# A four-batch decoder kernel: shorter weight loads and early splits, step products beside a norm, the recurrent mixer as one block, expert weights spread from bf16 rows

## The reference, cut to what matters

```python
x = _layernorm(x + _L0_attn_ref(x, ...))                  # selective-state scan, 1024 channels x 16 states
x = _layernorm(x + _L0_xattn_ref(x, fside, ctx_1024))     # two int8-style quantised linears
x = _layernorm(x + _L0_ffn_ref(x, ...))                   # silu(gate) * up, down, hidden 2048
x = _layernorm(x + _L1_attn_ref(x, ...))                  # recurrent mixer, 32 heads of 8 x 16 states
x = _layernorm(x + _L1_xattn_ref(ctx_1024, x, ...))       # selective-state scan, 512 channels x 16 states
x = _layernorm(x + _L1_ffn_ref(x, ...))                   # 8 routed experts of 352 and a shared one of 1408
```

```python
mus = einsum('blnr,nrd->blnd', tanh((x + delta * mu_x) @ Wx1), Wx2)     # five mixes
r = (x + delta * mr) @ Wr;  k = ... @ Wk;  v = ... @ Wv;  g = ... @ Wg
w = tanh((x + delta * mw) @ Ww1) @ Ww2 + bw;  decay = exp(-exp(w))
S = S * dt[..., :, None] + kv                                           # over 512 times
```

## Time and profile before

| | us |
|---|---|
| median of 3 runs | 4110.94 (4108.12 to 4114.24) |
| the profiled execution's own time | 4114.88 |
| its span, first to last instruction | 4113.1 |
| PE matmul / DVE / ACT / POOL busy in the span | 3610.2 / 3202.9 / 1641.1 / 1277.0 |
| mean granted PE clock | 0.935 |

### The profile page before, as it was taken

The page is one execution under the profiler, slowest core; times in us unless marked ns, Lnnn a source line. Parts: engine busy times, 40 slices in busy tenths (PEclk is TensorE's granted clock), DMA queues, the critical chain, the costliest instruction groups (busy, mean ns, idle before and its releaser), DMA issues. The chain is left out here.

```text
span 4113.1 us, 42098 instructions
## 1 busy us (share of the span) xinstructions
PE 3610.2 (88%) x15651; PEld 1499.2 (36%) x15651; DVE 3202.9 (78%) x2747; ACT 1641.1 (40%) x2207; POOL 1277.0 (31%) x453
## 2 busy tenths in 40 slices
PE   5777779978999979988999979988999979966999
PEld 2222243323433443323433443334333443323444
DVE  5998559768899869868899869778999869775333
ACT  4666443214655343214655353214655343112001
POOL 1444204343244304343244304343344304331000
PEclk9888899989899989989999999989999989977999
DMA  3888502222233402222233302122233302110222
GB/s 148 304 323 298 226 24 77 69 80 82 74 102 96 141 34 77 69 80 82 75 103 102 134 34 85 63 83 78 85 102 101 138 29 77 62 54 16 93 98 74
DMA packets 91354, 418.57 MB, mean 102 GB/s; under 512 B 14224, under 2 KB 26640, under 8 KB 88720
## 3 DMA queue, kind: packets, MB, share of 16 engines
q1 hardware_dynamic: 69552, 378.15, 26.0%
q10 hardware_dynamic: 21600, 37.73, 3.3%
HBM read 320.45 MB, written 70.25 MB: 95 GB/s over the span
## 5 line engine op out<-in xcount | busy, mean ns | idle before, releaser
L276 PE MATMUL ps<-r,ring 128*128 128x512 bf16 (+2 forms) x2040 | 786.5, 386 | 0.0
L1127 POOL TENSOR_TENSOR hh<-hh,bc 128x2048 f32<-128x2048 f32 x72 | 338.5, 4701 | 920.5 <-DVE hh L1047 920.5
L273 PE MATMUL ps<-xr,ring 128*128 128x512 bf16 x1568 | 614.9, 392 | 1.3 <-DVE r L259 1.2
L277 PE MATMUL ps<-xr,ring 128*128 128x512 bf16 x1568 | 613.7, 391 | 0.0
L273 PE MATMUL ps<-r,ring 128*128 128x512 bf16 (+2 forms) x1384 | 548.5, 397 | 63.7 <-DVE xc L1085 15.1
L277 PE MATMUL ps<-r,ring 128*128 128x512 bf16 (+2 forms) x1384 | 548.8, 397 | 0.0
L1127 POOL TENSOR_TENSOR bc<-bc 128x2048 f32<-128x2048 f32 x64 | 297.4, 4647 | 356.1 <-DVE bc L1047 356.1
L1127 POOL TENSOR_TENSOR r<-r,bc 128x2048 f32<-128x2048 f32 x56 | 263.1, 4699 | 325.2 <-DVE r L1047 325.2
L1047 DVE TENSOR_TENSOR_SCAN hh<-da,hh 128x2048 f32<-128x2048 f32 x72 | 330.1, 4585 | 1.3
L1088 DVE TENSOR_TENSOR xc<-xc,ps 128x512 f32<-128x512 f32 x176 | 119.4, 678 | 233.5 <-PE ps L277 233.5
L1047 DVE TENSOR_TENSOR_SCAN bc<-da,bc 128x2048 f32<-128x2048 f32 x64 | 289.6, 4525 | 0.5
(11 more groups left out here) (252 smaller groups left out, 6606.1 us busy)
## 6 DMA issues: line engine op xcount, KB each, us to landing
ring<-wsplit SPq DMA_DIRECT2D x304, 768.0 KB, 4.2
r<-wstream SPq DMA_DIRECT2D x76, 768.0 KB, 6.9
wsplit<-ring SPq DMA_DIRECT2D x58, 768.0 KB, 4.6
da<-r ACTq DMA_DIRECT2D x360, 63.9 KB, 2.0
wsplit<-r SPq DMA_DIRECT2D x18, 768.0 KB, 5.6
r<-xT SPq DMA_DIRECT2D x7, 1024.0 KB, 5.0
r<-gates_dram ACTq DMA_DIRECT2D x3, 2048.0 KB, 9.4
bc<-guwT SPq DMA_DIRECT2D x4, 1024.0 KB, 7.7
```

The costliest lines, as they stand in the source:

```text
L273: mm = pe.matmul(out, w_hi, x_hi, start=start, stop=False)
L276: pe.matmul(out, w_hi, x_lo, start=False, stop=False)
L277: return pe.matmul(out, w_lo, x_hi, start=False, stop=stop)
L1127: pool.tensor_tensor(quartet(s), quartet(s), k.out_rows, ALU.mult).then_inc(read, 1)
```

## The change

1. Used columns. `SLOT_COLUMNS` gives for each slot how many of its 1536 columns are used (1384 on average); ring loads, splitting and stores take only these. In `first_preparation` 8 of the 71 slots (9728 columns) are now split beside the preparation: ACT makes the high parts between its other steps, POOL all the low parts. 63 slots (88256 columns instead of 71 x 1536 = 109056) stay for the first scan stage, by DVE for 21 of them (28224 columns instead of 24 x 1536 = 36864) and PE for 42 (60032 columns in 118 chunks instead of 47 slots in 141).
2. Step products. `dt_product`, `magnitude`, `positive`, `exponential`, `logarithm`, `total` and the eight spread rows of the second scan leave `second_preparation` and go into `norm_and_steps`, which takes the place of `layer_norm` ln1 (and has no `keep_busy`).
3. One block for the mixer. `mix_inputs`, `mix_projections` and `mix_scan` become `mix_batch`. The scan loop starts after two of the four v products; the other two, the four g products and the 16 of the next batch are handed out in the loop, 3, 2, 3, 3, 2, 3, 3 and 3 in its eight steps. The third mix has tiles of its own (`xc`, `held_more`).
4. Weight rows. The expert weights' rows lie as three bf16 parts in 96 partitions, made on POOL at the start of "moe" (four instructions); a spread is one bf16 matmul over 96 rows instead of one f32 matmul over 32, and the first one comes after the first tile's gate and up.

```diff
-                sp.dma_start(self.whole[n % SPLIT_RING], self.source[self.slots[n]]).then_inc(self.landed[n % SPLIT_RING], 16)
+                at = slice(0, self.columns[n])
+                sp.dma_start(self.whole[n % SPLIT_RING][:, at], self.source[self.slots[n]][:, at]).then_inc(self.landed[n % SPLIT_RING], 16)
...
-def first_preparation(nc, k, slot, last):
+def first_preparation(nc, k, slot, last, splitter):
...
+                if j < SPLIT_RING:
+                    splitter.high_part(act, j)
             s.silu(act, J0 - 1)
             s.take_low(act)
             for j in range(J0):
                 s.magnitude(act, j)
+                if j % 2 == 1 and SPLIT_RING + j // 2 < count:
+                    splitter.high_part(act, SPLIT_RING + j // 2)
...
+            for n in range(early):
+                splitter.low_part(pool, n)
             for j in range(J0):
                 s.split_x(pool, j)
+            for n in range(early, count):
+                splitter.low_part(pool, n)
...
-                pe.matmul(weight_bank(e)[a:b, :], k.ident[q:q + 32, q + e:q + e + 1].broadcast_to([32, b - a]),
-                          k.weight_rows[q:q + 32, :], start=True, stop=True).then_inc(spread_mm, 1)
+                pe.matmul(weight_bank(e)[a:b, :], k.stack[0:96, e:e + 1].broadcast_to([96, b - a]),
+                          k.weight_parts, start=True, stop=True).then_inc(spread_mm, 1)
...
+def norm_and_steps(nc, k, tag, parts, slots_end, last):
...
+        @blk.tensor
+        def _(pe):
+            s.dt_product(pe, 0)
+            s.dt_product(pe, 1)
+            norm.means(pe)
+            s.dt_product(pe, 2)
+            s.dt_product(pe, 3)
+            norm.variances(pe)
+            for r in range(2 * GRP):
+                s.spread_row(pe, r)
...
+        @blk.vector
+        def _(dve):
+            norm.sums(dve)
+            s.positive(dve, 0)
+            s.positive(dve, 1)
+            norm.centred(dve)
+            s.positive(dve, 2)
+            s.positive(dve, 3)
+            for r in range(GRP):
+                s.dve_row(dve, r)
+            norm.scaled(dve)
+            for i in range(2):
+                s.total(dve, i)
...
+            value(0)
+            value(1)
             spread(0)
             pe.wait_ge(rb, 2)
...
+            work = [(value, 2), (value, 3)] + [(gate, o) for o in range(4)] + ([(ahead_product, n) for n in range(2 * J0)] if ahead else [])
+            given = 0
             for g in range(G):
                 if g + 1 < G:
                     spread(g + 1)
                 if g >= 1:
                     reduce(g - 1)
-                if ahead:
-                    project(2 * g)
-                    project(2 * g + 1)
+                until = max(len(work) * (g + 1) // G, min(3, len(work)))
+                for which, n in work[given:until]:
+                    which(n)
+                given = until
             reduce(G - 1)
...
+            times(0)
+            times(1)
+            split(0)
+            times(2)
+            split(1)
+            times(3)
+            dve.wait_ge(taken, 3)
+            low(dve, k.lowrank_lo, k.lowrank).then_inc(lsplit, 1)
+            split(2)
+            times(4)
+            split(3)
```

629 lines of the change are left out of this document (334 added, 295 removed).

## The result

| | before | after |
|---|---|---|
| median of the runs, us | 4110.64 (4108.12 to 4114.24, 4 runs) | 3986.22 (3982.17 to 3991.31, 4 runs) |
| span of the profiled execution | 4113.1 | 3980.4 |
| PE matmul / DVE / ACT / POOL busy | 3610.2 / 3202.9 / 1641.1 / 1277.0 | 3521.7 / 3172.7 / 1609.0 / 1378.0 |
| mean granted PE clock | 0.935 | 0.939 |

The ratio is 0.9693, 95% interval 0.9681 to 0.9706. The time forecast was 3981.

What follows compares the result with a forecast made beforehand. Bounds were taken by stage: DVE in the first scan stage and mixer loop, PE in "moe", engines waiting in turn in the mixer's front. Terms 8 - 26 - 37 - 16 + 43 - 58 - 30 - 14 = -130 gave 3981 us, range 3938 to 4030.

Steps and rivals of the forecast that it cites:

- The sum: Whole kernel: all terms together -130 us, giving 3985 in a profiled execution and 3981 as median.
- The second preparations and the norm: Step products move to ln1: second preparations -37 (batches two to four) and -16 (first), four norms +43 us.
- the 20 dummy matmuls were hidden: In ln1: the 20 dummy matmuls that go were hidden, so no term was given for removing them.
- The first scan stage: Fewer slots and 19% fewer columns for DVE, PE and ACT: -26 us, between -10 and -45.
- The first preparation: ACT and POOL split eight slots there, POOL's low parts meeting DVE's taps: +8 us, between +1 and +20.
- The front of the mixer: Mixer before its first scan: multiplications a mix early bring that scan to 54.8 from 86.1 us, -31.
- The loop: Mixer scan loop with a next batch: becomes PE's and ends after 80 instead of 69 us.
- in DVE's slack: Mixer with a next batch: POOL's four low parts of the next x cost about 1 us, in DVE's slack.
- the last batch: Last batch's mixer: loop stays DVE's, first scan at 54.8, 126 instead of 156.1 us, -30 (-20 to -35).
- The weight rows: "moe": bf16 spreads over 96 rows give -2 us in each stage with a scan, -8 in the last, together -14.
- the front keeps its pace: Rival, mixer front: low parts and POOL's additions lock each other out, front 12 us longer, +48, 4029; chance 0.14.
- The lower clock for a whole loop: Rival, mixer loop: PE at the lower clock, products 5.1 instead of 2.76 us, 4135 in all; chance 0.04.

Runs made afterwards that it cites:

- e3: The changed kernel with the step products and spread rows back in the second preparation and the plain norm in their place; 3991.46 us, ratio 0.9704.
- e10: The changed kernel with 30 dummy matmuls behind the spread rows of the norm with the step products; 3989.72 us, ratio 0.9699.
- e1: The changed kernel with all 1536 columns used in every slot again; 3998.21 us, ratio 0.9715.
- e2: The changed kernel with no slot split in the first preparation, all 71 split in the first scan stage; 4008.04 us, ratio 0.9738.
- e7: The changed kernel with the multiplications of each mix directly ahead of its low parts, not a mix early; 4033.07 us, ratio 0.9805.
- e8: The changed kernel with one matmul instead of three for each part of the next batch's 16 products in the mixer loop; 3966.35 us, ratio 0.9642.
- e5: The changed kernel with the low parts of the next batch's x made by DVE ahead of the first mixer scan, not by POOL; 4012.92 us, ratio 0.9753.
- e4: The changed kernel with the expert weights' rows spread in f32 from 32 rows again, without POOL's splitting; 4010.52 us, ratio 0.9743.
- e6: e5 with the second product of v also moved into the mixer loop; 4021.53 us, ratio 0.9773.
- e9: The changed kernel with POOL splitting x after its reads, DVE's read directly behind the scan, and the second v product in the loop; 4008.20 us, ratio 0.9747.
- e11: The changed kernel with both e9's mixer loop order and e10's dummy matmuls; 3985.18 us, ratio 0.9693.

## Why the prediction was right, step by step

*The sum* is nearer than its terms: against the forecast the first preparation came out 5.0 lower and "moe" 7.3 lower, the mixers 9.0 and the first scan stage 1.6 higher. That these cancel to 2.7 is luck; each mechanism below is judged by its own stage. (The profiled execution is also the fastest of the four: the median is 5 above the forecast.)

*The second preparations and the norm* were right to 1.6 us a batch (13.2, 13.2 and 10.6 for 12.2; that they sum to the forecast's 37 is luck too) and to 0.1 in the norm, because all of it was counted from rows of these stages: 36 products at 5.52 for 24, ACT's functions and DVE's four operations by name. What was wrong is the sentence that the 20 dummy matmuls were hidden: they cost nothing where they stood, but the stage behind them pays for their absence (177.7 for 176.0 to 177.6 before and 176.0 to 177.5 in e3, part of it back in e10).

*The first scan stage* came out at -24.4 for -26. From scan to scan it takes 10.0 us in its first half and 10.4 in its second (10.3 and 11.6 before), which was to come under 10.6. e1 and e2 show that the parts had other sizes: the eight early slots give 14.5, the narrower columns 7.4.

*The first preparation* was oversized, +3.0 for +8. POOL's 19.6 us were priced as four pieces in the way of DVE's taps and 3.5 us of ACT; in fact they met little: DVE's busy time grew by 3.6, and POOL's is 30.5, 2.0 more than its 8.95 of before and the 19.6. "SBUF — State Buffer" of the Trainium skill, section "Who interferes with whom", would let DVE pay for the whole of POOL's work where the two meet throughout; here it paid less than a fifth of it.

*The front of the mixer* came as forecast, 53.0 for 54.8, but the sum behind it counted DVE alone. PE makes 150 matmuls there without a gap from 1699.55 to 1737.4, about 10 us of it at the low clock, and DVE is nearly as full. e7 shows the part of the early multiplications, 15.9 us (8.7 of waits, 7.2 at the lower clock of e7's front); the rest of the 33.1 is about six products of 2.76, those of v and g that left the front (this part is worked out, no run shows it). The clock over the front is 0.90 for 0.85 before, which the forecast did not count.

*The loop* is the term that was mis-sized: 85.2 for 80. That it would be PE's is shown by e8, and the 5 us that PE was to wait in the first two steps are 12.1 (85.2 less 73.07). POOL's four low parts of x were costed at 1 us "in DVE's slack"; with them its first read ends 17.5 us after the scan's start, and PE waits 6.0 for it. In e5 and e7, where they aren't in the loop, PE's idle time is 7.7 and 7.6. But e3 shows that they need not cost this where they stand: with the same instructions and a first scan 2.4 later, PE has no such wait and the loop is 81.3, near the forecast. In the last batch the loop is 76.5 for 73.5, by DVE's own reads of the first two steps, 3.15 and 2.41 for 1.23, which meet POOL's. For this batch the forecast also added wrongly: 54.8 and its loop of 71 + 2.5 are 128.3, not 126, so -27.8 and not -30; the measured -26.8 is nearer to its terms than to its sum.

*The weight rows* are worth 16.4 (e4) for 14. The traces differ by 21.3; the other 5 us are not from the rows and lie in the three stages with a scan (350.3 in e4 for 351.3 to 352.2 before); where they are from wasn't tried.

Of the rivals, "the front keeps its pace" did not come, although what spoke for it did: POOL's additions are stretched to 9.5 us, but only for the last mix, when DVE has nothing left that waits for them before the scan. The lower clock for a whole loop did not come (0.94 in it); the low stretch of 10 us in the front was there before too.

What stays open: how the moment of a stage decides whether PE's clock falls in it. It is seen, not controlled; no run here moved a stage without changing a program.

## What to carry to other kernels

When a block is fused so that two engines' work lies side by side, count every engine's sum over the new block, and look at the first steps of a loop by themselves: the wait of 6.0 us that the forecast missed is behind four small operations on the idlest engine. Measure before moving them: no order tried here (e5, e6, e9) made the mixer with a next batch clearly shorter. When work is moved in one engine's queue, find its reader in the other's and move that too. And judge an edit worth less than a few tenths of a per cent by its stage, in the execution, not by the time of the whole.

## What the runs showed that was not expected

PE's granted clock falls in stretches with no idle PE in the rows (0.64 over the 12 us of e9 above), and whether it does depends on more than the instructions: the same mixer takes 137.9 or 140.3 within one execution of e9, the same norm 28.8 or 25.6 within one of e1, the same last mixer 129.3 or 132.5. Over a whole program this makes some 20 us (e9's 4008.20 and e11's 3985.18 differ in their instructions by the 30 dummies in four norms alone, and the FFN stages of e11 gain nothing from them in sum), more than most single edits here were worth. And DVE can hold up POOL: POOL's four additions take 9.5 to 9.9 us for 5.85 where DVE's operations follow each other without a gap, and one of them in the changed kernel's front takes 5.3 by itself, where most take 1.3 to 1.7.
